# One more key block of each set turned by VectorE, with fewer visits of TensorE to the attends, in a four-layer graph network

## The reference

```
q, k, v = x @ Wq + bq, x @ Wk + bk, x @ Wv + bv          # (n, 4, 32)
attn  = einsum('nhc,mhc->hnm', q, k) / sqrt(32)
e     = where(adj == 0, 0, exp(attn - rowmax))
alpha = e / sum(e)
out   = einsum('hnm,mhc->hnc', alpha, v)
x_r   = x @ Ws + bs
beta  = sigmoid(concat([out, x_r, out - x_r]) @ Wb)
x     = layernorm(x + beta * x_r + (1 - beta) * out)
```

## Time and profile before

| | |
|---|---|
| median of three runs | 1787.44 us |
| the profiled execution | 1787.36 us, its span 1785.7 us |
| busy over the span | PE 1738.2, PEld 1131.9, DVE 1228.2, ACT 975.7, POOL 895.6 us |
| turns by PE, line 739 | 3592 transposes, 485.5 us |
| attends, line 760 | 8192 passes, 276.7 us |
| scores, line 698 | 1024 matmuls, 353.9 us |
| masks on DVE, line 1278 | 512 |
| exponentials on ACT, line 973 | 256, 516.2 us |

### The profile page before, as it was taken

The page is one execution under the profiler, slowest core; times in us unless marked ns, Lnnn a source line. Parts: engine busy times, 40 slices in busy tenths (PEclk is TensorE's granted clock), DMA queues, the critical chain, the costliest instruction groups (busy, mean ns, idle before and its releaser), DMA issues.

```text
span 1785.7 us, 40361 instructions
## 1 busy us (share of the span) xinstructions
PE 1738.2 (97%) x15000; PEld 1131.9 (63%) x15000; DVE 1228.2 (69%) x2405; ACT 975.7 (55%) x1505; POOL 895.6 (50%) x849
## 2 busy tenths in 40 slices
PE   7999999999998899999999999999999999999996
PEld 3444444444444677877877877778778777644442
DVE  4777775222125889999999999999999999301322
ACT  0110111010002798999999999999999999411101
POOL 0211111111114755778878789788787896540211
PEclk9999999999999999999999999999999999999998
DMA  9866766799996645445445445454454553797991
GB/s 373 318 222 253 253 251 234 275 315 402 374 389 223 222 146 170 155 155 158 157 149 166 146 163 162 163 166 157 143 182 141 162 164 115 311 370 273 327 325 61
DMA packets 138637, 396.92 MB, mean 222 GB/s; under 512 B 16224, under 2 KB 66656, under 8 KB 113888
## 3 DMA queue, kind: packets, MB, share of 16 engines
q1 hardware_dynamic: 117504, 356.83, 57.1%
q10 hardware_dynamic: 18720, 30.42, 4.8%
q0 software_dynamic: 2240, 7.34, 1.4%
HBM read 333.19 MB, written 61.34 MB: 221 GB/s over the span
## 4 chain that ended last, share of the span: by engine, by line
PE 88%; DMA 4%; DVE 3%; issue 1%; SPq 1%; ACT 1%; POOL 1%; ACTq 0%; DVEq 0%; POOLq 0%
PE bank L588 32%; PE bank L739 22%; PE bank L760 14%; PE bank L698 13%; DMA q_dram<-arena 2%; DVE arena L1278 1%; DMA arena<-adj_cols 1%; PE bank L576 1%; PE bank L609 1%; PE bank L610 1%; PE bank L651 1%; PE bank L603 0%; PE bank L766 0%; SPq L396 0%; DMA arena<-adj 0%
## 5 line engine op out<-in xcount | busy, mean ns | idle before, releaser
L973 ACT ACTIVATE arena<-arena,small 128x2048 f32<-128x2048 f32 x256 | 516.2, 2017 | 2.5 <-DVE small L1278 2.5
L739 PE MATMUL bank<-ident,arena 128*128 128x128 f32 x3592 | 485.5, 278 | 4.4 <-ACT arena L973 2.8
L739 PEld LDWEIGHTS bank<-ident,arena 128*128 128x128 f32 x3592 | 398.2, 141 | 87.7 <-issue 42.1
L588 PE MATMUL bank<-arena,stat_s 128*128 128x512 f32 x1008 | 439.4, 593 | 4.0 <-DVE arena L1245 1.9
L985 ACT ACTIVATE arena<-bank 128x512 f32<-128x512 f32 x673 | 377.1, 604 | 66.8 <-PE bank L739 66.2
L698 PE MATMUL bank<-k,parts 128*128 128x512 f32 x1024 | 353.9, 435 | 10.9 <-DVE small L1278 10.8
L588 PEld LDWEIGHTS bank<-arena,stat_s 128*128 128x128 f32 x1008 | 189.2, 190 | 229.1 <-issue 227.7
L760 PE MATMUL bank<-arena,stat_x 128*32 128x128 f32 x8192 | 276.7, 276 | 0.4 <-DMA arena<-group_dram 0.4
L760 PEld LDWEIGHTS bank<-arena,stat_x 128*32 128x32 f32 x8192 | 208.0, 109 | 91.5 <-issue 81.6
L588 PE MATMUL bank<-arena,stat_x 128*128 128x512 f32 x512 | 229.8, 600 | 10.3 <-DMA arena<-adj_cols 8.0
L698 PEld LDWEIGHTS bank<-k,parts 128*128 128x128 f32 x1024 | 158.9, 192 | 29.5 <-DVE small L1278 24.2
(11 more groups left out here) (155 smaller groups left out, 1432.0 us busy)
## 6 DMA issues: line engine op xcount, KB each, us to landing
arena<-adj_cols SPq DMA_DIRECT2D x190, 1024.0 KB, 6.6
stat_s<-adj SPq DMA_DIRECT2D x85, 512.0 KB, 4.7
group_dram<-stat_s SPq DMA_DIRECT2D x63, 512.0 KB, 2.9
arena<-group_dram SPq DMA_DIRECT2D x252, 128.0 KB, 2.8
arena<-adj SPq DMA_DIRECT2D x43, 512.0 KB, 4.7
parts<-q_dram SPq DMA_DIRECT2D x128, 64.0 KB, 2.4
k_dram<-arena ACTq DMA_DIRECT2D x28, 256.0 KB, 7.3
q_dram<-arena ACTq DMA_DIRECT2D x28, 256.0 KB, 11.8
```

Of the source, the lines that this page charges most:

```text
L588: mm_ = pe.matmul(bank[:, to, :], stat[:, jt, :], ring[:, s, j, :], start=(jt == 0), stop=(jt == TILES - 1))
L739: last = pe.transpose(bank[:, b_, h * P:(h + 1) * P], cols[:, st % SETS, h, u * P:(u + 1) * P], ident[:, :])
L973: act.activation(cols[:, s_, h, :], cols[:, s_, h, :], ACT.Exp, bias=shift[:, t % 2, 1, i:i + 1], scale=-1.0, accum_out=blocksum[:, t % 2, ...
```

## The change

A third unit of each set, unit 13, is turned in blocks by DVE, so PE turns 13. The turns stand at places 1, 2 and 6, and the group is three units. PE attends in three visits a set, at places 4, 8 and 14, with four, six and six units. DVE copies 23 units a chunk and ACT 81, at newly listed places; most of the 32 exponentials of a chunk stand one to three places elsewhere. A chunk's two last `post_steps` (of the row after) stand two places later.

The room for it comes from the buffers: two mask buffers instead of three, masks loaded 7 ahead; the group lands in a region of its own in `stat_s`, no longer in turn slots, so its load waits for the attends of the set before; and six chunks of `xt` (0 to 5) go through memory. PE's last product waits for all six before it starts. `load_xt` also waits for the last group's attends.

```
-ATTEND_BATCH = 4
-ATTEND_LAG = 8
-BLOCK_TURN_AT = {14: 3, 15: 5}
-GROUPS = ((14, 15),)
+ATTENDS = {4: (-4, -3, -2, -1), 8: (0, 1, 2, 3, 4, 5), 14: (6, 7, 8, 9, 10, 11)}
+BLOCK_TURN_AT = {13: 1, 14: 2, 15: 6}
+GROUPS = ((13, 14, 15),)
...
-MASK_AHEAD = 8
-MASKS = 3
-SPILLED = (2, 3, 4, 5)
+MASK_AHEAD = 7
+MASKS = 2
+SPILLED = (0, 1, 2, 3, 4, 5)
...
-        adj_in = (arena[:, RING + 4 * CHUNK:RING + 6 * CHUNK], spilled[:, 0:2 * CHUNK], spilled[:, 2 * CHUNK:4 * CHUNK])
+        adj_in = (arena[:, RING + 4 * CHUNK:RING + 6 * CHUNK], spilled[:, 0:2 * CHUNK])
+        group_slots = spilled[:, 2 * CHUNK:5 * CHUNK]
...
-                if g * UPS + GROUPS[i][-1] >= TURNED:
-                    sp.wait_ge(unit_used, g * UPS + GROUPS[i][-1] - TURNED + 1)
+                if g > 0:
+                    sp.wait_ge(unit_used, (g - 1) * UPS + GROUPS[i][-1] + 1)
...
+                sp.wait_ge(unit_used, GROUP_SETS * UPS)
                 for i in range(len(SPILLED)):
                     sp.wait_ge(xt_out, 16 * (i + 1))
...
-            load_mask(0, 4)
             sp.wait_ge(gcn_k_out, 64 * CHUNKS)
...
-            load_mask(0, 5)
+            load_mask(0, 4)
             sp.wait_ge(gcn_dve, CV(last, "root"))
             sp.dma_start(root_dram[:, last * CHUNK:CHUNKS * CHUNK], root_out).then_inc(gcn_root_out, 16)
-            for m in range(6, MASK_AHEAD):
+            for m in range(5, MASK_AHEAD):
                 load_mask(0, m)
...
-                    if (k - ATTEND_LAG) % ATTEND_BATCH == 0:
-                        for a in range(k - ATTEND_LAG, k - ATTEND_LAG + ATTEND_BATCH):
-                            if a >= 0:
+                    for a in attended_at(c, k):
+                        if a >= 0:
...
-            product(2, 0, {0: [final_out], SPILLED[0] - 1: [lambda: pe.wait_ge(xt_in_place, 16 * len(SPILLED))], 5: [lambda: pe.wait_ge(att_pool, AG(last - 1, "xt"))],
+            pe.wait_ge(xt_in_place, 16 * len(SPILLED))
+            product(2, 0, {0: [final_out], 5: [lambda: pe.wait_ge(att_pool, AG(last - 1, "xt"))],
```

More of the change, by code:

```diff
@@ L122 @@
 LAST_UNITS = [k for k in range(UPC - UPS, UPC) if k % UPS in BLOCK_TURN_AT]
+LAST_BY_VECTOR, LAST_BY_SCALAR = LAST_UNITS[0::2], LAST_UNITS[1::2]
 def is_block_turned(c, k):
@@ L198, in last_bank_before, with attended_at, slot_of, used_before @@
     return TURN_BANKS.uses[LAST_USE + 1 + LAST_UNITS.index(k) - len(TURN_BANKS.BANKS)][1]
+def attended_at(c, k):
+    u = k % UPS
+    return [k - u + a for a in ATTENDS.get(u, ())]
+def slot_of(k):
+    return (PE_UNITS + LAST_UNITS).index(k) % TURNED
+def used_before(c, k):
+    i = (PE_UNITS + LAST_UNITS).index(k) - TURNED
+    return c * UPC + PE_UNITS[i] + 1 if i >= 0 else (c - 1) * UPC + PE_UNITS[i] + 1
 BY_VECTOR = [k for k in PE_UNITS if (k % 16 in VECTOR_PLACES or k in VECTOR_ALSO) and k not in VECTOR_NOT]
@@ L305, in slots_of @@
         def slots_of(i):
-            first, n = GROUPS[i][0] % TURNED - 6, len(GROUPS[i])
-            return group_slots[:, first * CHUNK:(first + n) * CHUNK]
+            return group_slots[:, 0:len(GROUPS[i]) * CHUNK]
         def tiles(ap):
@@ L758, in attend @@
                     else:
-                        weights = turned[k % TURNED][:, h * P:(h + 1) * P]
+                        weights = turned[slot_of(k)][:, h * P:(h + 1) * P]
                     last = pe.matmul(to, stat_x[:, k % UPT, h * C:(h + 1) * C], weights,
@@ L794, in attention @@
                             scores(*ahead, first and k < UPS)
[L795 to L800 removed]
+                    for a in attended_at(c, k):
+                        if a >= 0:
+                            attend(c, a, first)
+                        elif not first:
+                            attend(c - 1, UPC + a, False)
                     if not is_block_turned(c, k):
@@ L812, in attention @@
                 if last_chunk:
-                    for a in range(UPC - ATTEND_LAG, UPC):
+                    for a in range(UPC - 4, UPC):
                         attend(c, a, first)
@@ L1046, in attention @@
                         block_weights(c, k // UPT)
-                    if k in BY_SCALAR or (last_chunk and k == LAST_UNITS[1]):
+                    if k in BY_SCALAR or (last_chunk and k in LAST_BY_SCALAR):
                         copy_unit(c, k, first)
@@ L1374, in attention @@
             def attention(c, first, last_chunk):
-                post = post_steps(c - 1, 107 if last_chunk else 113) if not first else {}
+                post = post_steps(c - 1, 107 if last_chunk else 115) if not first else {}
                 for k in range(UPC):
@@ L1394, in attention @@
                             turn_blocks(c, k - place + u)
-                    if k in BY_VECTOR or (last_chunk and k == LAST_UNITS[0]):
+                    if k in BY_VECTOR or (last_chunk and k in LAST_BY_VECTOR):
                         copy_unit(c, k, first)
```

60 lines of the change are left out of this document (26 added, 34 removed).

## The result

The changed kernel takes 1810.22 us (median of 4 runs, 1807.16 to 1813.88) against 1786.99 for the kernel before (median of four, too): ratio 1.013, 95% interval 1.0118 to 1.0142. It is slower, 35 us over the forecast and above its range of 1758 to 1790. The profiled execution took 1812.27 us, its span is 1810.6.

The account below looks back on a forecast made before the run. PE was taken as the bound, with DVE and ACT within 6%. Chunk -24.5, group +1.5, start +3.5, end +4, clock +3.4 sum to -12.1 us: from 1787.44 to 1775 us, 8-in-10 range 1758 to 1790.

Parts of the forecast that it names:

- Masks: SP's mask loads with two buffers, 7 ahead: same POOL step awaited, each mask about 4.7 us later, nothing in mid-chunk.
- What would uncover it: Condition for a mid-chunk mask cost: POOL late by a set, SP then holding the group's store behind a mask load.
- the group is late: Rival: SP's store waits behind a mask load, stopping PE at place 4; 1 us in half the sets makes 1804; chance 0.08.
- The chunk of 116.6 us: Mid-chunk period forecast, from 119.87: gain 3.27 us a chunk over 7.5 chunks, -24.5 us.
- a period over 118.2: Sign that the forecast is wrong: once-a-chunk instructions more than 118.2 us apart, where 116.6 was expected.
- PE's price: PE's work per set: one turned unit less and three visits for four save 0.78 us, chunk 119.9 to 113.7.
- DVE as the bound: Rival: DVE already bounds, so its +2.4 us lengthens each chunk, giving 1818 us; chance 0.04.
- the misfit of PE and DVE: Rival: long visits and paired turns make PE and DVE stop each other; 118.5 us a chunk, 1790 us; chance 0.14.
- Start, +3.5: Attention's start: first group's store 2.1 to 3.6 us late behind mask loads, larger group about 1 us more; bounds 0 and 5.
- End, +4: Before PE's last product: all six `xt` loads must land first, ending at 1548 to 1550; +4 us, bounds 0 and 6.
- clock, +3.4: PE's granted clock drops behind the start and end waits, half of 6.8 us possible each; +3.4 us, bounds 0 and 6.8.
- The group, +1.5: Group's way through memory, hidden by a small margin before place 4; +1.5 us over the attention, bounds 0 and 30.

Follow-up runs that it names:

- store_ahead_in_set7: The changed kernel with the group's store ahead of the first mask load in each chunk's eighth set: 1808.7 us, ratio 1.0128.
- masks_by_pool: The changed kernel with another SP order at the end and masks from the third on loaded by POOL's own queue: 1856.0 us, ratio 1.0393.
- early_blend_load_first: Last and fastest run: the changed kernel, SP's order changed everywhere, sum y before the bias, group's load before the second mask load in third sets: 1776.6 us.

## Why the prediction was wrong

- **The step that failed is *Masks*: "nothing in mid-chunk".** Its first sentence holds: SP waits for the same POOL step. In the changed kernel POOL then waits 72 us for masks. I had measured the slack where DVE uses the biases, and asked whether a mask would come too late for it. None did. I didn't follow SP's queue between the moment a buffer is free and its load's issue (4.7 us in the rows above), nor what stands behind the waiting bias in POOL's program: the sums y and of h's squares, for which DVE waits 21.6 us in seven chunks once the kernel before has two buffers. There that alone costs 21 us, and SP's order gives 19 of them back. In the changed kernel the same cure (with the store first in set 0, too), on top of the other start and end, took 1791.7 to 1780.7 us.
- **What would uncover it** was named there: "POOL late by a set, and SP then holding the group's store behind a mask load". It needed far less than a set. Before, in the fitted order, the bias that releases the store of a chunk's eighth set ended about 1 us before the turn did; POOL has to be late by that much only. The rival *the group is late* has the right place and price (1804), and I gave it 0.08, for the store's 2.9 us and the margin at the load; the margin that counted was SP's release. It is still a symptom: with 2.3 us of group waits left the time was 1797.
- **The chunk of 116.6 us** was reached by no run; the best averages 118.7, and I had named a period over 118.2 as a sign of being wrong. PE's price isn't what failed: a set without waits lasts 14.17 us, as shown above. Neither DVE as the bound nor the misfit of PE and DVE explains the 35 us: the waits that runs could take away lead to POOL and SP. What is left in the best run is 2.1 us a chunk on average, with PE's 7.8 us of waits for the group in it, and 1.1 us even in its shortest period. No run takes that apart; the misfit, which I had priced at 118.5 us a chunk, isn't excluded for it. So 1776.6 near my 1775 is partly luck: the chunk gains (119.87 - 118.7) x 7.5 = 8.8 us instead of 24.5, and at the ends, which I had charged with 10.9, PE waits 0.85 us for `xt` and not at all for the first group. By the rule of the Trainium skill's page "Perfetto Trace Analysis", section "Identifying the Most-Contended Engine", which gave 1818, DVE was to be relieved first; in the changed kernel DVE is less busy than before in mid-chunk (112.0 against 113.4), so the time near that figure has another cause. Only the last kernel comes near to the rule's picture: DVE 116.44, weight loads 95.56.
- **Start, +3.5** (bounds 0 and 5): PE's wait grew by 5.9. Mask 4's load left at 590.48, right behind the queries' stores, as I had it. Counted from their end, the group's store left 3.7 us later than before, where I had 2.1 to 3.6, and the larger group took 1.8 us more from there to PE, where I had 1. The other 3.3 us of the 7.03 were there when the queries' stores ended; in store_ahead_in_set7, with the same start, these ended 0.5 us later than before, and PE waited 5.88 us all the same.
- **End, +4**: 5.80, inside the bounds; **clock, +3.4** for both: at the start alone the granted clock was 0.54 and 0.78 in the two stretches of 5 us behind the wait, (0.46 + 0.22) x 5 / 0.5 = 6.8 us at 1.2 GHz. PE works in some 5.8 of these and loses 2.9; the end adds 1.4 in the first slot. Five of the six mid-chunk waits have their own, for which I had nothing; behind the shortest, of 1.56 us, the clock stays at 1.00. Another order gave back 8.3 and 8.8 us at the two ends, where I had 10.9 for both.
- **The group, +1.5**: from 680 to 1500 us PE's row has no wait for it outside the eighth sets. For those, see above.

In sum: of 35 us between forecast and result about 5 are the ends (5.9 + 2.9 + 5.8 + 1.4 = 16.0 against 10.9). The rest is the chunk, 5.1 us over the forecast in each of six, with the waits for the group in it.

## What to carry to other kernels

Before a buffer is taken away, follow one free buffer to its next load: which waits and issues stand ahead of that load in its queue, and what stands behind the instruction that then waits, not only who uses the data. An order that was fitted to one period has its margins there (here 1 us in SP's release of a store); a change that shortens the period or adds a wait has to be tried with the order fitted anew, since it was the order, not the work, that made this one slow. And a wait that is taken away often shows up one queue further on, as in three of these runs.

## What the runs showed of the hardware that I had not expected

- A wait of PE in mid-chunk costs more than itself: behind 4.41 us without work the clock was granted at 0.50 for 5 us, as after the 6.30 us at the start (0.54) and around the 5.80 at the end (0.50). Behind the mid-chunk wait of 1.56 us it stayed at 1.00.
- A mask load issued by POOL takes 0.57 to 0.68 us of POOL (masks_by_pool), 0.9 with the wait for its own instruction; issued by SP the same load takes 0.35 to 0.43 us at the median, and up to 1.7, of a queue that computes nothing (the changed kernel).
- The time from issue to landing of the same store of 768 KB varies from 3.2 to 7.5 us within one execution (early_blend_load_first), and PE's longest wait in it, 3.0 us, stands behind the one of 7.5.
